# A linear-attention context stage on one core: the context product as four column quarters, and the strip's operand made in two parts

## The reference, cut to what matters

```
t = group_norm(x) as tokens                  # 12544 x 128, per image
q, k, v = t @ Wqkv + bqkv                    # 8 heads of 16 channels
q = relu(q) * scale;  k = relu(k)
ctx = einsum('bhnd,bhne->bhde', k, v)        # 16x16 for each head, summed over all tokens
out = einsum('bhnd,bhde->bhne', q, ctx)      # then depthwise 3x3, projection, MLP, two norms
```

## Time and profile before

| | |
|---|---|
| median of 3 runs | 2789.6 us (2786.65 to 2791.28) |
| the profiled execution | 2789.54 us, its span 2787.7 us |
| busy share of the span | PE 94%, PEld 78%, DVE 81%, ACT 77%, POOL 49% |
| mean granted TensorE clock | 0.981 |
| context stage | from about 1170 to 1411 us of the span |

### The profile page before, as it was taken

How to read it: one execution, slowest core, us unless ns; L and a number is a source line. 1 busy time by engine, 2 the same in 40 slices (tenths; PEclk the granted TensorE clock), 3 DMA queues, 4 the chain that set the end, 5 groups by cost and what they waited for, 6 DMA issues and landing times.

```text
span 2787.7 us, 76479 instructions
## 1 busy us (share of the span) xinstructions
PE 2615.0 (94%) x28138; PEld 2176.2 (78%) x28138; DVE 2267.2 (81%) x5003; ACT 2134.8 (77%) x3921; POOL 1369.2 (49%) x1322
## 2 busy tenths in 40 slices
PE   2999899999999999899979999999999999999999
PEld 2777777777777777699968888888888888888887
DVE  4888788878888888577778888888888888888885
ACT  1677677767776777455569999999999999999997
POOL 1445445545555555345525555555555555554554
PEclk9999999999999999899989999999999999999999
DMA  4222122212221111133301111111011111100000
GB/s 137 66 67 79 54 81 71 73 55 87 66 72 42 53 53 40 50 124 114 116 24 41 40 37 40 40 41 39 31 40 40 40 40 38 39 27 20 20 19 22
DMA packets 55758, 151.60 MB, mean 54 GB/s; under 512 B 6608, under 2 KB 20944, under 8 KB 55632
## 3 DMA queue, kind: packets, MB, share of 16 engines
q1 hardware_dynamic: 55632, 149.93, 16.7%
HBM read 98.52 MB, written 51.38 MB: 54 GB/s over the span
## 4 chain that ended last, share of the span: by engine, by line
PE 86%; ACT 6%; DVE 3%; issue 3%; DMA 1%; POOL 1%; SPq 0%; DVEq 0%; POOLq 0%; ACTq 0%
PE bank L1255 14%; PE bank L1257 14%; PE bank L1256 13%; PE bank L1487 12%; PE bank L1320 7%; PE bank L1308 7%; ACT prob L663 5%; PE bank L1408 5%; PE bank L1416 3%; PE bank L1334 3%; PE bank L1328 2%; PE bank L1244 2%; PE bank L1289 2%; PE bank L1304 1%; DMA ximg<-x_in 1%
## 5 line engine op out<-in xcount | busy, mean ns | idle before, releaser
L598 POOL TENSOR_TENSOR hl<-hf,hh 128x448 fp32r<-128x448 f32 x448 | 517.5, 1155 | 637.9 <-ACT hh L791 637.9
L1139 DVE SCALAR_TENSOR_TENSOR bank<-oring,dw,bank 128x448 f32<-128x448 f32 x896 | 614.8, 686 | 20.1
L1487 PE MATMUL bank<-hw,w 128*128 128x448 f32 x896 | 391.2, 538 | 0.0
L1255 PE MATMUL bank<-t1h,w_hi 128*128 128x448 f32 x896 | 364.9, 407 | 6.0 <-DVE t1l L1156 6.0
L788 ACT ACTIVATE hf<-bank,fc1b 128x448 f32<-128x448 f32 x448 | 282.5, 631 | 111.8 <-PE bank L1257 111.8
L1257 PE MATMUL bank<-t1l,w_hi 128*128 128x448 f32 x896 | 325.7, 364 | 0.0
L1256 PE MATMUL bank<-t1h,w_lo 128*128 128x448 f32 x896 | 323.0, 360 | 0.0
L1320 PEld LDWEIGHTS bank<-vx,prob 128*64 128x64 f32 x6272 | 205.8, 140 | 98.8 <-issue 83.5
L791 ACT ACTIVATE hh<-hf 128x448 fp32r<-128x448 f32 x448 | 259.2, 578 | 14.1
L782 ACT ACTIVATE hw<-bank,fc1b 128x448 f32<-128x448 f32 x448 | 265.9, 618 | 0.4 <-PE bank L1257 0.4
L663 ACT ACTIVATE prob<-bank 128x512 f32<-128x512 f32 x448 | 207.4, 549 | 75.9 <-PE bank L1308 75.9
(11 more groups left out here) (156 smaller groups left out, 6865.7 us busy)
## 6 DMA issues: line engine op xcount, KB each, us to landing
ximg<-x SPq DMA_DIRECT2D x112, 448.0 KB, 3.4
ximg<-x_in SPq DMA_DIRECT2D x56, 448.0 KB, 3.4
x<-ximg SPq DMA_DIRECT2D x56, 448.0 KB, 2.5
y_out<-yb SPq DMA_DIRECT2D x112, 224.0 KB, 1.9
xs<-x_in SPq DMA_DIRECT2D x42, 448.0 KB, 3.4
wm<-wm_in SPq DMA_DIRECT2D x1, 512.0 KB, 3.7
w1f<-w_in SPq DMA_DIRECT2D x1, 512.0 KB, 5.4
w<-w_in SPq DMA_DIRECT2D x1, 512.0 KB, 7.1
```

Source lines behind the costliest of these rows:

```text
L598: g.tensor_tensor(hl[:, k, :], hf[:, k % 2, :], hh[:, k, :].bitcast(F32), ALU.subtract).then_inc(hl_ready, 1)
L1139: m = d.scalar_tensor_tensor(acc, src, dw[:, k:k + 1], acc, ALU.mult, ALU.add)
L1255: mm(out, w[0], x[0], start=start, stop=False)
L1487: m = mm(out, w2[:, j, :], hw[:, WHOLE_J.index(j), :], start=first, stop=last)
```

## The change

The context product of a token tile is taken as four products of 32 columns of k with 32 columns of v, one for each column quarter, which write 32x32 results to the four partition quarters of the bank. The eight 16x16 blocks on the diagonal are inside these four; the mask is applied to a broadcast read of the 32 columns. The products of a whole strip stand together, after the second chunk of the next strip's projections, behind one wait for the strip's last relu. `kv` holds two strips, and the relu is done in place in it; `krel` is gone. A wait of `lkv` on the addition that read its bank a strip earlier is now written out, where the wait for the relu implied it.

The norm, the rounding and the subtraction are done in two parts, of 4 and 3 token tiles (`STRIP_PARTS`), each with its own count: DVE issues them after the second and the fourth chunk of a strip, for the strip after next; ACT rounds each part behind the relu of the same chunk; POOL subtracts each part.

```diff
+QUAD = P // QUADS
+STRIP_PARTS = ((0, 4 * P), (4 * P, STRIP - 4 * P))
+NP = len(STRIP_PARTS)
...
-        kv = sb("kv", [P, 4, 2, 2, P])
-        krel = sb("krel", [P, 4, 2, P])
+        kv = sb("kv", [P, 2, 4, 2, 2, P])
...
                     for sp in range(2):
-                        pool.wait_ge(tsth_ready, h * 2 + (sp + 1))
-                        g.tensor_tensor(tstl[:, sp, :], tfull[:, sp, :], tsth[:, sp, :].bitcast(F32),
-                                        ALU.subtract).then_inc(tstl_ready, 1)
+                        for k, (c0, n) in enumerate(STRIP_PARTS):
+                            c = slice(c0, c0 + n)
+                            pool.wait_ge(tsth_ready, h * (2 * NP) + (sp * NP + k + 1))
+                            hold(pool)
+                            g.tensor_tensor(tstl[:, sp, c], tfull[:, sp, c], tsth[:, sp, c].bitcast(F32),
+                                            ALU.subtract).then_inc(tstl_ready, 1)
...
+            def high_part(S, sp, k):
+                c0, n = STRIP_PARTS[k]
+                act.wait_ge(tfull_ready, S * NP + k + 1)
+                a.activation(tsth[:, sp, c0:c0 + n], tfull[:, sp, c0:c0 + n], ACT.Copy).then_inc(tsth_ready, 1)
...
+                    act.wait_ge(kv_ready, S * len(KV_CHUNKS) + cc + 1)
+                    a.activation(kv[:, sp, cc, 0:n, 0, :], kv[:, sp, cc, 0:n, 0, :], ACT.Relu)\
                         .then_inc(krel_ready, 1)
+                    if more and cc % 2 == 1:
+                        high_part(S + 2, sp, cc // 2)
...
+                if not (i == 0 and isinstance(h, int) and h == 0):
+                    dve.wait_ge(tstl_ready, (i * STRIPS + s - 2) * NP + k + 1)
                 hold(dve)
-                if not (i == 0 and isinstance(h, int) and h == 0):
-                    dve.wait_ge(tstl_ready, i * STRIPS + s - 1)
-                d.tensor_scalar(tfull[:, sp, :], ximg[:, bass.ds(s * STRIP, STRIP)], gc[:, 1, i, 0:1],
+                d.tensor_scalar(tfull[:, sp, c0:c0 + n], ximg[:, bass.ds(s * STRIP + c0, n)], gc[:, 1, i, 0:1],
                                 gc[:, 1, i, 1:2], ALU.mult, ALU.add).then_inc(tfull_ready, 1)
...
+                    if ahead and cc % 2 == 1:
+                        norm_part(*ahead, sp, cc // 2)
...
+            def contexts(i, S, sp, first=False, last=False):
+                pe.wait_ge(krel_ready, S * NK + NK)
+                for cc, (_, n) in enumerate(KV_CHUNKS):
+                    for t in range(n):
+                        for j in range(QUADS):
+                            c = slice(QUAD * j, QUAD * j + QUAD)
+                            m = mm(bank[6 + i % 2][c, 0:QUAD], kv[:, sp, cc, t, 0, c], kv[:, sp, cc, t, 1, c],
+                                   start=(first and cc == 0 and t == 0), stop=(last and cc == NK - 1 and t == n - 1),
+                                   skip_group_check=True)
                 m.then_inc(ctx_mm, 1)
...
-                pe.wait_ge(tsth_ready, S + 1)
                 for cc in range(NK):
+                    if cc % 2 == 0:
+                        pe.wait_ge(tsth_ready, S * NP + cc // 2 + 1)
+                    if not (start and i == 0):
+                        pe.wait_ge(kv_ready, S * NK + cc - NK + 1)
                     lkv(S, sp, cc)
...
+                    if cc == CTX_LAG - 1:
+                        if not start:
+                            if isinstance(s, int) and s == 1 and i > 1:
+                                pe.wait_ge(ctxm_ready, i * 3 - 3)
+                            contexts(i, S - 1, 1 - sp, first=(isinstance(s, int) and s == 1))
+                        elif i > 0:
+                            contexts(i - 1, S - 1, 1 - sp, last=True)
```

More of the change, by code:

```diff
@@ L712, in _, with strip_c @@
             group_loop(act, step, prologue, epilogue)
[L715 to L719, removed]
+            def high_part(S, sp, k):
+                c0, n = STRIP_PARTS[k]
+                act.wait_ge(tfull_ready, S * NP + k + 1)
+                a.activation(tsth[:, sp, c0:c0 + n], tfull[:, sp, c0:c0 + n], ACT.Copy).then_inc(tsth_ready, 1)
+            def strip_c(S, sp, more=True):
                 for cc, (_, n) in enumerate(KV_CHUNKS):
-                    K = S * len(KV_CHUNKS) + cc
-                    act.wait_ge(kv_ready, K + 1)
-                    a.activation(krel[:, cc, 0:n, :], kv[:, cc, 0:n, 0, :], ACT.Relu)\
+                    act.wait_ge(kv_ready, S * len(KV_CHUNKS) + cc + 1)
+                    a.activation(kv[:, sp, cc, 0:n, 0, :], kv[:, sp, cc, 0:n, 0, :], ACT.Relu)\
                         .then_inc(krel_ready, 1)
-            high_strip(0, 0)
-            with act.Fori(0, NIMG * STRIPS // 2 - 1) as h:
[L729 to L735, removed]
+                    if more and cc % 2 == 1:
+                        high_part(S + 2, sp, cc // 2)
+            for S in range(2):
+                for k in range(NP):
+                    high_part(S, S, k)
+            with act.Fori(0, NIMG * STRIPS // 2 - 1) as h:
+                for sp in range(2):
+                    strip_c(h * 2 + sp, sp)
+            for sp in range(2):
+                strip_c(NIMG * STRIPS - 2 + sp, sp, more=False)
             def tb_high(B, bb):
@@ L1037, in _, with norm_part, strip_c @@
             group_loop(dve, step, prologue, epilogue)
-            def norm_strip(i, h, sp):
+            def norm_part(i, h, sp, k):
                 s = h * 2 + sp
[L1043 to L1046, removed]
+                c0, n = STRIP_PARTS[k]
+                if k == 0:
+                    if i == 0:
+                        dve.wait_ge(xb_loaded, ((NIMG - 1) * STRIPS + s + 1) * 16)
+                    else:
+                        dve.wait_ge(xl_loaded[sp], ((i - 1) * (STRIPS // 2) + h + 1) * 16)
+                    hold(dve)
+                if not (i == 0 and isinstance(h, int) and h == 0):
+                    dve.wait_ge(tstl_ready, (i * STRIPS + s - 2) * NP + k + 1)
                 hold(dve)
-                if not (i == 0 and isinstance(h, int) and h == 0):
-                    dve.wait_ge(tstl_ready, i * STRIPS + s - 1)
-                d.tensor_scalar(tfull[:, sp, :], ximg[:, bass.ds(s * STRIP, STRIP)], gc[:, 1, i, 0:1],
+                d.tensor_scalar(tfull[:, sp, c0:c0 + n], ximg[:, bass.ds(s * STRIP + c0, n)], gc[:, 1, i, 0:1],
                                 gc[:, 1, i, 1:2], ALU.mult, ALU.add).then_inc(tfull_ready, 1)
-            def strip_c(S):
+            def strip_c(S, sp, ahead=None):
                 for cc, (_, n) in enumerate(KV_CHUNKS):
@@ L1059, in strip_c @@
                         .rearrange("p (a b) c -> p a (b c)", a=1).to_broadcast([P, n, 2 * P])
-                    d.tensor_tensor(kv[:, cc, 0:n].rearrange("p t b c -> p t (b c)"), src, bias,
+                    d.tensor_tensor(kv[:, sp, cc, 0:n].rearrange("p t b c -> p t (b c)"), src, bias,
                                     ALU.add).then_inc(kv_ready, 1)
+                    if ahead and cc % 2 == 1:
+                        norm_part(*ahead, sp, cc // 2)
             def context_masked(i):
-                dve.wait_ge(ctx_mm, (i + 1) * (STRIPS * len(KV_CHUNKS)))
+                dve.wait_ge(ctx_mm, (i + 1) * STRIPS)
                 if i > 0:
                     dve.wait_ge(ctxm_ready, i * 3)
-                d.tensor_tensor(ctxm[:], bank[6 + i % 2][:, 0:P], cmat("cmask"), ALU.mult).then_inc(ctxm_ready, 1)
+                quads = bank[6 + i % 2][:, 0:QUAD].rearrange("p (j c) -> p j c", j=1).to_broadcast([P, QUADS, QUAD])
+                d.tensor_tensor(ctxm[:].rearrange("p (j c) -> p j c", j=QUADS), quads,
+                                cmat("cmask").rearrange("p (j c) -> p j c", j=QUADS), ALU.mult).then_inc(ctxm_ready, 1)
                 dve.wait_ge(ctxm_ready, i * 3 + 1)
@@ L1076, in _ @@
             dve.wait_ge(gcoef_ready, NIMG + 1)
-            norm_strip(0, 0, 0)
-            norm_strip(0, 0, 1)
+            for sp in range(2):
+                for k in range(NP):
+                    norm_part(0, 0, sp, k)
             for i in range(NIMG):
@@ L1081, in pair @@
                     for sp in range(2):
-                        strip_c(i * STRIPS + h * 2 + sp)
-                        if i == 0 and isinstance(h, int) and h == 0 and sp == 0:
-                            strip_stats(NIMG - 1, STRIPS - 1, NG)
+                        ahead = None
                         if not (isinstance(h, int) and h == STRIPS // 2 - 1):
-                            norm_strip(i, h + 1, sp)
+                            ahead = (i, h + 1)
                         elif i + 1 < NIMG:
@@ L1089, in pair @@
                                 dve.wait_ge(gcoef_ready, NIMG + 2)
-                            norm_strip(i + 1, 0, sp)
+                            ahead = (i + 1, 0)
+                        strip_c(i * STRIPS + h * 2 + sp, sp, ahead)
+                        if i == 0 and isinstance(h, int) and h == 0 and sp == 0:
+                            strip_stats(NIMG - 1, STRIPS - 1, NG)
```

(7 more changed lines are left out.)

2 lines of the change are left out of this document (1 added, 1 removed).

## The result

The changed kernel took 2800.85 us (median of 6 runs) where the kernel before took 2790.44: a ratio of 1.0048 with an interval of 1.0026 to 1.0071. It is 10 us slower; 35 us faster was forecast, and the time lies outside the range. The product became shorter about as expected, and the stage still lost time. The profiled execution has a span of 2798.9 us, 11.2 more than before.

The account below looks back on a forecast made before the run. The prediction took TensorE's own pace, 4.05 us a strip, as the context stage's bound. A 3.42 us step saves 0.63 us on 55 strips, 35 us: 2789.6 - 35 = 2755 us, range 2743 to 2786.

Parts of the forecast that it names:

- What bounds the kernel before: Context stage: bound by TensorE's own pace, 4.05 us a strip, of which 1.56 us are the product.
- The product in quarters: TensorE's context product: four quarters side by side, weights then columns in turn, 42 ns a step, 0.59 us a strip.
- The two switches: TensorE, array shape changed before and after the product: 0.09 going in, 0.10 + 0.05 coming back, 0.24 us a strip.
- TensorE's strip: TensorE in the context stage: 2.49 + 0.59 + 0.24 = 3.32 us a strip instead of 4.05.
- The ring over the relus: Product, third chunk, DVE's additions, last relu, hand-overs: 3.27 us a strip, barely hidden under TensorE's 3.32.
- DVE's parts: DVE's norm split into 512 and 384 elements: 538 + 470 ns, adding 264 ns a strip.
- The sum for DVE: DVE's additions and norm parts: 3.51 us a strip if nothing overlaps, above 3.32, making DVE a joint bound.
- Rival (1): Context stage: only two quarters run at once, or one DVE part is slowed by 0.40 us; 2782 us, chance 0.12.
- the middle of 3.42: The strip's forecast step, taken between TensorE's 3.32 and DVE's 3.51 us, saving 0.63 us a strip.
- POOL's runs "will meet DVE's more often": POOL's subtraction, 2.1 us a strip, gains at most a few tenths: hidden, though meeting DVE's runs more often.
- Start, borders and end at nothing: Start, image borders and end of the stage: each changes by less than 1 us, left at nothing.

Follow-up runs that it names:

- e9: e4_gate with the 56 product instructions of a strip ordered by column quarter, all 14 of one before the next; 2799.28 us, 1.0035 of the kernel before.
- e4_gate: The changed kernel with one more wait: POOL subtracts a part only when DVE has ended the following norm part; 2744.86 us, 0.984 of the kernel before.
- e1: The changed kernel, but POOL subtracts only 8 columns of each part, the rest of the low operand left out; 2744.36 us, 0.9837 of the kernel before.
- e5_mid: The kernel before with column quarters, one whole norm after a strip's second chunk for the strip after next, rounding after the fourth relu; 2797.04 us, 1.0024.

## Why the prediction was wrong

- **What bounds the kernel before**: read rightly; TensorE alone, 4.05 us.
- **The product in quarters, 42 ns for four, 0.59 us**: the quarters run side by side, as said, but the price was too high. The 56 take 0.70 us, less 0.20 for the last one 0.50, over 13.75 steps of four: 36 ns a step in the mean, and mostly 32 or 33 in the single starts. Weights and then columns in turn, 0.46 and 0.86 ns a column, is wrong: by it a quarter's pace is 42 ns, and e9 has 31 to 32. What fits the rows better is the larger of the two numbers of columns at 0.87 ns, to within 4 ns: L1308 with 128 and 64 has 112, L1416 with 128 and 128 has 111, L1320 with 64 and 34 has 60, the new shape with 32 and 32 has 32. This is an estimate; no run changed one number alone.
- **The two switches, 0.24 us; TensorE's strip 3.32 us**: right in the sum. Chain and step in e4_gate have 3.31. There the product starts 0.21 us after the last projection where neighbours are 0.12 apart, the next projection starts 0.63 us after the product, and the one behind it 0.22 later: 0.09 + 0.63 + 0.10 = 0.82 us beside the 2.49, where 0.59 + 0.24 = 0.83 was forecast. That it agrees so closely is in part luck, since the product was priced by a wrong split.
- **The ring over the relus, 3.27 us, just hidden**: right. In e4_gate TensorE waits for the relus three times between 1250 and 1380 us, 2.4 us in all, and not from strip to strip.
- **DVE's parts, 538 + 470 ns**: as costs right (0.54 and 0.47 in e1), and this is the step that failed. The sum for DVE, 3.51 us, had no term for a wait of the norm parts for POOL; the forecast put it at nothing. Rival (1) named the place and took L1113's 1023 ns beside L1118's 619 for POOL's doing. But it was priced at one part and 0.40 us, and then discounted since "L1050 is an operation with one tensor and kept 744 on average". It kept 744 because no subtraction ran beside it: the old order had norm, rounding, subtraction in a row, and the next norm came when POOL was through. What the average stood for was the schedule, which the change replaces. And the guess on L1113 could be tested in the trace before: 107 of its 112 begin beside POOL's L598 and take 1.04 us in the median, ending 0.48 after it; the five others take 0.62 or 0.63. The runs showed 0.38 and 1.01 us of waiting, 1.39 a strip; DVE's 3.0 us of work became 4.38. Without the waits DVE is no bound of its own: the step in e4_gate is TensorE's 3.31, not the middle of 3.42.
- **POOL's runs "will meet DVE's more often"**: said, and not followed to the end. With the parts made in the middle of the strip there is a ring of norm part, rounding, subtraction and next part, and a ring does not drift apart: each held-up part moves the next subtraction onto the next part.
- **Start, borders and end at nothing**: good to about 5 us. From the first addition to the last strip's first, the stage took 13.6 us longer, where 55 x 0.33 would be 18. The difference lies where the steps are other than 4.38, at the ends of the stage and the image borders; how it divides I did not work out.

That the change costs 10 us is thus not one small effect but two large ones: 0.74 us a strip gained on TensorE and 1.07 us lost to the ring (4.38 less 3.31).

## What to carry to other kernels

Before moving or splitting an operation on DVE, look at what POOL runs at its new moment, not at the mean of its old one; an instruction that again and again ends a fixed time after another engine's has ended, whenever it began, is waiting for that engine inside its busy time. A wait that puts the two in turn can be worth more than the work that it delays: here it was 56 us, for one added wait. And when a small part lasts longer than a large one, the first experiment is to shorten the other engine's work.

## What the runs showed of the hardware that I had not expected

- A busy DVE can be an idle one: 153.86 of 154 us count as busy, of which 1.39 in each 4.38 us were the wait for POOL.
- The exclusion goes by whole instructions and by who is first: 0.01 us later costs the norm part 1.01 us, while 0.15 us earlier cost the other engine 0.45 (e5_mid).
- The first quarter of a microsecond of a norm part can lie beside a subtraction at no cost: 0.26 us in e4_gate. Only what lies deeper inside is paid for.
- f32 products of 128x32 weights and 32 columns, in four column quarters in turn, started every 9.1 ns in the mean (0.50 us / 55), and within one quarter every 31 to 32 ns. The rule of about 25 ns between starts is in the Trainium skill, "TensorE: Matmul & The Clock Gate", Part 1. The trace disagrees with it across four quarters; within one quarter the starts are further apart than 25 ns, so nothing here tests it.
